# A competitive attention whose residual moves to ScalarE, whose counts are applied in the transposed copy, and whose steps stand in another order

## The reference, cut to what matters

```
x = x + tanh(g_xattn[1]) * L1_xattn(layernorm(x), ctx, alpha, beta)

def L1_xattn(X, C, alpha, beta):
    sim = sigmoid(beta + alpha * einsum('bkd,btd->bkt', C, X))
    mask = one_hot(argmax(sim, axis=1), K, axis=1)         # each token picks one context row
    agg = einsum('bkt,btd->bkd', sim * mask, X) + C         # what the tokens bring to their row
    out_k = agg / (sum(mask, axis=-1) + 1)                  # divided by one plus the count of tokens
    return X + einsum('bkt,bkd->btd', sim, out_k)
```

## Time and profile before

| what | value |
|---|---|
| time of 3 runs, median (lowest to highest) | 1693.77 us (1693.45 to 1694.56) |
| time of the profiled execution | 1691.46 us |
| span of its records | 1689.7 us |
| granted TensorE clock, mean of the span | 0.925 of full speed |
| busy share PE, VectorE, ScalarE, GpSimd | 83%, 64%, 40%, 46% |
| the phase | from about 453 to 557 us |

### The profile page before, as it was taken

One profiled execution on the slowest core, in us unless ns is written; L12 is line 12 of the kernel. 1 busy time (PEld: TensorE's weight loads), 2 busy tenths in 40 slices (PEclk: granted clock), 3 DMA queues, 4 the chain that ended last, 5 costly groups with the idle time before them and its releaser, 6 DMA issues. The chain is left out here.

```text
span 1689.7 us, 34140 instructions
## 1 busy us (share of the span) xinstructions
PE 1406.0 (83%) x10919; PEld 1116.2 (66%) x10919; DVE 1081.6 (64%) x2418; ACT 681.7 (40%) x1663; POOL 780.9 (46%) x1037
## 2 busy tenths in 40 slices
PE   4999765989656785999978886899999999687996
PEld 3777655989655564666634444777878778587884
DVE  4888752414399687999958884455555855364455
ACT  3676442323343333556633332344455454421121
POOL 2554581345384353555533331444444577307355
PEclk9999897999855897999979999899999999889899
DMA  6400015758110000000000000000000000186952
GB/s 183 179 2 2 11 34 158 220 170 265 54 33 10 1 1 1 0 0 0 0 1 0 0 0 1 1 0 0 0 1 1 6 20 15 54 235 188 275 163 83
DMA packets 96487, 100.03 MB, mean 59 GB/s; under 512 B 12150, under 2 KB 69678, under 8 KB 95727
## 3 DMA queue, kind: packets, MB, share of 16 engines
q1 hardware_dynamic: 62322, 69.60, 13.6%
q0 software_dynamic: 8192, 16.79, 3.4%
q10 hardware_dynamic: 25852, 12.09, 2.5%
HBM read 72.23 MB, written 26.21 MB: 58 GB/s over the span
## 5 line engine op out<-in xcount | busy, mean ns | idle before, releaser
L439 POOL TENSOR_TENSOR exp_scores<-exp_scores,softmax_recip 128x308 f32<-128x308 f32 x256 | 181.7, 742 | 179.8 <-DVE softmax_recip L611 179.6
L633 PE MATMUL psum<-identity,exp_scores 128*77 128x128 f32 x1024 | 164.7, 287 | 37.6 <-POOL exp_scores L439 25.4
L1942 POOL TENSOR_TENSOR exp_scores_xattn<-exp_scores_xattn,softmax_recip_xattn 128x1640 f32<-128x1640 f32 x32 | 93.5, 2921 | 162.6 <-DVE softmax_recip_xattn L2115 162.6
L1201 PE MATMUL psum<-sorted_transposed_ffn,tile_weights_up_ffn 128*128 128x128 f32 x1280 | 164.7, 283 | 4.3 <-DVE sorted_transposed_ffn L1089 4.1
L633 PEld LDWEIGHTS psum<-identity,exp_scores 128*77 128x77 f32 x1024 | 123.2, 153 | 60.5 <-issue 28.9
L1201 PEld LDWEIGHTS psum<-sorted_transposed_ffn,tile_weights_up_ffn 128*128 128x128 f32 x1280 | 154.1, 197 | 11.6 <-DVE sorted_transposed_ffn L1089 11.4
L975 POOL DMA_INDIRECT gathered_rows_ffn<-sorted_y,slot_ffn x96 | 90.7, 944 | 105.4 <-DMA sorted_y<-expert_rows_ffn 46.4
L454 ACT COPY probs_transposed<-psum 77x512 f32<-77x512 f32 x192 | 111.2, 581 | 57.3 <-PE psum L633 55.4
L1211 PE MATMUL psum<-expert_weights_down_ffn,hidden_ffn 128*128 x960 | 123.7, 280 | 3.3 <-issue 2.9
L964 POOL DMA_INDIRECT sorted_x<-xn_ffn,slot_ffn x64 | 61.3, 957 | 139.3 <-DVE slot_ffn L851 120.4
L1211 PEld LDWEIGHTS psum<-expert_weights_down_ffn,hidden_ffn 128*128 128x128 f32 x960 | 115.8, 195 | 5.2 <-issue 5.2
(11 more groups left out here) (367 smaller groups left out, 3388.7 us busy)
## 6 DMA issues: line engine op xcount, KB each, us to landing
tile_weights_up_ffn<-in_L_ffn_packed_dram SPq DMA_DIRECT2D x160, 256.0 KB, 3.3
sorted_rows_ffn<-sorted_x SPq DMA_DIRECT2D x80, 128.0 KB, 3.7
sorted_y<-expert_rows_ffn ACTq DMA_DIRECT2D x80, 128.0 KB
sorted_x<-zeros SPq DMA_DIRECT2D x4, 1280.0 KB, 13.0
x_residual<-in_x_dram SPq DMA_DIRECT2D x4, 512.0 KB, 11.3
expert_weights_down_ffn<-in_L_ffn_packed_dram SPq DMA_DIRECT2D x8, 256.0 KB, 15.2
sorted_x<-xn_ffn,slot_ffn POOLq DMA_INDIRECT x128, 2.2
gathered_rows_ffn<-sorted_y,slot_ffn POOLq DMA_INDIRECT x128, 2.9
```

The costliest lines, as they stand in the source:

```text
L439: nc.gpsimd.tensor_tensor(e[:, par, heads, :], e[:, par, heads, :], rec.to_broadcast([S, HG, KC]), ALU.mult).then_inc(s["probs_ready"], 1)
L633: last = nc.tensor.transpose(m.psum[0:KC, 4 + g % 2, h * S:(h + 1) * S], e[:, nxt, g * HG + h, :], m.ident[:, :])
L1201: mm = nc.tensor.matmul(m.psum[:, 2 * (n % 2) + half, to:to + SUB], w[:, n % DEPTH, u, at:at + 128], xst[:, n % 2, u * SUB:(u + 1) * SUB], ...
L1942: nc.gpsimd.tensor_tensor(ev, ev, recip[:, par, :].unsqueeze(2).to_broadcast([S, H3, KV]), ALU.mult).then_inc(s["probs_ready"], 1)
```

## The change

Four things are changed. (1) GpSimd no longer forms gate x xn and adds it. Since xn is rstd x x + shift, x + gate x xn is (1 + gate x rstd) x x + gate x shift; VectorE makes the two columns from rstd and shift (`moves`), and ScalarE applies them to x in place, right behind xn and for the group that it just normalised. (2) VectorE no longer multiplies `rows` by the reciprocal counts. ScalarE applies these as a scale while it copies the transposed sim out of PSUM: the counts belong to the partitions there, but differ by batch, so the one copy becomes four ACTIVATEs; it also moves behind the copy of the transposed xn. (3) On VectorE the small steps on the counts stand between the steps of the picks, and `combine` stands ahead of adding y to x. (4) On PE the transposes of sim stand ahead of the aggregation.

```diff
-                        wait(pool, s["x_moved"], g)
-                        nc.gpsimd.tensor_tensor(gated[:, :], xn[:, par, :, :].rearrange("p b d -> p (b d)"), m.gate[:, 1:2].to_broadcast([S, GB * D]),
-                                                ALU.mult).then_inc(s["xn_used"], 1)
-                        wait(pool, s["xn_used"], g + 1)
-                        xg = m.x[:, bass.ds(g * GB, GB), :].rearrange("p b d -> p (b d)")
-                        nc.gpsimd.tensor_tensor(xg, xg, gated[:, :], ALU.add).then_inc(s["x_moved"], 1)
...
                     if front:
                         wait(act, s["xt_in_psum"], g)
-                        wait(act, s["xn_used"], g)
+                        wait(act, s["weighted_ready"], g)
...
-                    if back:
-                        wait(act, s["simt_in_psum"], g)
-                        wait(act, s["y_done"], g - 1)
-                        nc.scalar.copy(simt[:, :], m.psum[0:KC, 2, :]).then_inc(s["simt_ready"], 1)
+                        wait(act, s["xn_ready"], g + 2)
+                        for t in range(GB):
+                            at = (g + 1) * GB + t
+                            ins = nc.scalar.activation(m.x[:, at, :], m.x[:, at, :], ACT.Identity, scale=move_scale[:, bass.ds(at, 1)],
+                                                       bias=move_shift[:, bass.ds(at, 1)])
+                        ins.then_inc(s["x_moved"], 1)
                     if front:
                         wait(act, s["xt_in_psum"], g + 2)
                         wait(act, s["z_in_psum"], g)
                         nc.scalar.copy(xt[:, nxt, :], m.psum[:, 0, :]).then_inc(s["xt_ready"], 1)
+                    if back:
+                        wait(act, s["simt_in_psum"], g)
+                        wait(act, s["y_done"], g - 1)
+                        wait(act, s["back_link"], (g - 1) * BACK + 2)
+                        for t in range(GB):
+                            ins = nc.scalar.activation(simt[:, t * S:(t + 1) * S], m.psum[0:KC, 2, t * S:(t + 1) * S], ACT.Identity,
+                                                       scale=tally[:, t // 2, t % 2:t % 2 + 1])
+                        ins.then_inc(s["simt_ready"], 1)
...
+                def moves(lo, hi):
+                    nc.vector.tensor_scalar(move_scale[:, lo:hi], m.rstd[:, lo:hi], gate, 1.0, ALU.mult, ALU.add).then_inc(s["moves_ready"], 1)
+                    nc.vector.tensor_scalar(move_shift[:, lo:hi], m.shift[:, lo:hi], gate, None, ALU.mult).then_inc(s["moves_ready"], 1)
...
-                        nc.vector.tensor_tensor(rows[:, :, :], rows[:, :, :], tl.unsqueeze(2).to_broadcast([KC, GB, D]), ALU.mult)\
-                            .then_inc(s["back_link"], 1)
...
+                    if g >= 0:
+                        combine(g)
                     if back:
                         wait(dve, s["y_done"], g)
                         wait(dve, s["x_moved"], g)
...
                         for t in range(GB):
                             nc.vector.bn_stats(m.moments[:, (g - 1) * GB + t, :], m.x[:, (g - 1) * GB + t, :])
-                    if g >= 0:
-                        combine(g)
...
                     if back:
+                        wait(pe, s["sim_ready"], g)
+                        wait(pe, s["simt_ready"], g - 1)
+                        for t in range(GB):
+                            mm = nc.tensor.transpose(m.psum[0:KC, 2, t * S:(t + 1) * S], sim[:, nxt, t, :], m.ident[:, :])
+                        mm.then_inc(s["simt_in_psum"], 1)
                         wait(pe, s["pick_ready"], g)
                         wait(pe, s["weighted_ready"], g)
...
                         mm.then_inc(s["agg_in_psum"], 1)
-                        wait(pe, s["simt_ready"], g - 1)
-                        for t in range(GB):
-                            mm = nc.tensor.transpose(m.psum[0:KC, 2, t * S:(t + 1) * S], sim[:, nxt, t, :], m.ident[:, :])
-                        mm.then_inc(s["simt_in_psum"], 1)
```

More of the change, by code:

```diff
@@ L1302, in competitive_attention @@
     names = ("parts_ready var_ready sd_ready rstd_ready shift_ready neg_ready ones_ready xn_ready xt_in_psum xt_ready "
-             "z_in_psum exp_ready one_added xn_used x_moved best_ready weighted_ready sim_ready pick_ready simt_in_psum simt_ready agg_in_psum y_done x_done mid_link back_link late_first late_combined late_moments")
+             "z_in_psum exp_ready one_added moves_ready x_moved best_ready weighted_ready sim_ready pick_ready simt_in_psum simt_ready agg_in_psum y_done x_done mid_link back_link late_first late_combined late_moments")
     s = {n: sem(f"{n}_1") for n in names.split()}
     gate = m.gate[:, 1:2]
-    MID, BACK = 3, 4
+    MID, BACK = 3, 3
     FIRST = 4
@@ L1328, in competitive_attention @@
         code = sb("pick_code", [S, GB])
-        gated = sb("gated_xn", [S, GB * D])
+        move_scale, move_shift = sb("one_plus_gated_rstd", [S, B]), sb("gated_shift", [S, B])
         weighted = sb("weighted_tokens", [S, 2, GB, D + 1])
@@ L1376, in _ @@
                 act.wait_ge(s["neg_ready"], 1)
-                act.wait_ge(s["shift_ready"], 1)
+                act.wait_ge(s["moves_ready"], 2)
                 def step(g, par, front, middle, back):
@@ L1385, in step @@
                         preload(nc, m, ACT.Exp)
-                        act.wait_ge(s["shift_ready"], before + 1)
+                        act.wait_ge(s["moves_ready"], 2 * before + 2)
                     if front:
                         wait(act, s["xt_in_psum"], g)
-                        wait(act, s["xn_used"], g)
+                        wait(act, s["weighted_ready"], g)
                         for t in range(GB):
@@ L1446, in step @@
                         rstd_of_x(nc, m, dve, s["sd_ready"], s["rstd_ready"], s["shift_ready"], lo, hi, before)
+                        moves(lo, hi)
                     link_m = chain(dve, s["mid_link"], g, MID)
@@ L1452, in step @@
                         nc.vector.reciprocal(sv, sv).then_inc(s["sim_ready"], 1)
+                    agg = m.psum[0:KC, 3:5, 0:2 * (D + 1)].rearrange("p j (u c) -> p j u c", u=2)
                     if back:
                         wait(dve, s["agg_in_psum"], g)
-                        wait(dve, s["y_done"], g - 1)
-                        agg = m.psum[0:KC, 3:5, 0:2 * (D + 1)].rearrange("p j (u c) -> p j u c", u=2)
+                        wait(dve, s["simt_ready"], g - 1)
                         nc.vector.tensor_scalar(tally[:, :, :].unsqueeze(3), agg[:, :, :, D:D + 1], 1.0, None, ALU.add).then_inc(s["back_link"], 1)
-                        nc.vector.tensor_tensor(rows[:, :, :].rearrange("p (j u) d -> p j u d", u=2), agg[:, :, :, 0:D],
-                                                m.ctx[:, bass.ds((g - 1) * GB, GB), :].rearrange("p (j u) d -> p j u d", u=2), ALU.add)\
-                            .then_inc(s["back_link"], 1)
-                        wait(dve, s["back_link"], (g - 1) * BACK + 2)
-                        nc.vector.reciprocal(tl, tl).then_inc(s["back_link"], 1)
-                        wait(dve, s["back_link"], (g - 1) * BACK + 3)
-                        nc.vector.tensor_tensor(rows[:, :, :], rows[:, :, :], tl.unsqueeze(2).to_broadcast([KC, GB, D]), ALU.mult)\
-                            .then_inc(s["back_link"], 1)
                     if middle:
@@ L1470, in step @@
                         nc.vector.tensor_reduce(best[:, par, :], sv, AX.X, ALU.max).then_inc(s["best_ready"], 1)
+                    if back:
+                        wait(dve, s["back_link"], (g - 1) * BACK + 1)
+                        nc.vector.reciprocal(tl, tl).then_inc(s["back_link"], 1)
+                    if middle:
                         wait(dve, s["best_ready"], g + 1)
@@ L1474, in step @@
                         link_m(nc.vector.tensor_tensor(pv, sv, best[:, par, :].unsqueeze(2).to_broadcast(wide), ALU.is_ge))
+                    if back:
+                        wait(dve, s["y_done"], g - 1)
+                        nc.vector.tensor_tensor(rows[:, :, :].rearrange("p (j u) d -> p j u d", u=2), agg[:, :, :, 0:D],
+                                                m.ctx[:, bass.ds((g - 1) * GB, GB), :].rearrange("p (j u) d -> p j u d", u=2), ALU.add)\
+                            .then_inc(s["back_link"], 1)
+                    if middle:
                         link_m(nc.vector.tensor_tensor(pv, pv, m.down[:, 0:KC].unsqueeze(1).to_broadcast(wide), ALU.mult))
```

1 line of the change is left out of this document (added).

## The result

The changed kernel took 1684.53 us (median of 5, 1681.15 to 1686.09) against 1693.45 (5, 1691.23 to 1694.56): ratio 0.9947, 95% interval 0.9931 to 0.9962. It is 8.9 us faster, where 10.3 (1683.5 us) had been worked out.

What follows compares the result with a forecast made beforehand. The phase was read as VectorE's time line, with 12.3 us standing still for GpSimd. Terms 7.45 + 2.1 - 0.1 + 0.8 + 0.45 - 0.24 - 0.2 gave 10.3 us less: 1683.5 us at the median, range 1679.5 to 1690.

Steps and rivals of the forecast that it cites:

- Rival 3: In rounds 1, 2, 4 any GpSimd work, gathers too, holds VectorE; 4.65 us would come back: 1688.2 us; 9%.
- rival 5: In rounds 1 to 4 combine operations are held beside their round's gathers, up to 22.8 us: 1706 us, slower; 5%.
- Rounds 0, 1, 2, 4: 12.2 us of holds, combine and small steps go, 4.75 stay or come: 7.45 us saved.
- Round 4's race: Comparison against GpSimd's L1356: 0.15 us of hold stays if comparison starts first, 0.95 if not; middle 0.55 taken.
- The wait for gathers in round 1: With combine ahead of L1482, VectorE comes for the sixth gather at 8.6, it lands at 10.0: 1.4 us wait.
- Round 3: VectorE does its combine inside the wait for PE; round falls from 11.98 to 9.9 us: 2.1 saved.
- Round 5: Hangs on the same chain to y as round 3, but has no combine: 0.1 us lost.
- Round 7: Scaled copies take 1.2 us, y is late next; round takes 7.65 us: 0.8 saved.
- Round 6: PE has all its work at the low clock, 8.0 us: 0.45 saved from 8.45.
- Rival 2: PE goes to 2.4 GHz in late rounds as it becomes denser, some 4 us: 1679.5 us; 12%.
- Start and tail: First copy 0.24 us later; tail's aggregation behind four transposes and y, 0.2 us lost.
- the rule weighed in the prediction: VectorE instructions with two SBUF inputs and GpSimd instructions reading SBUF exclude one another; the first issued keeps the other out.

Runs made afterwards that it cites:

- Experiments 1: Kernel before with only the residual moved from GpSimd to ScalarE, old steps and order kept: 1689.74 us, ratio 0.9974.
- 3: Changed kernel with two GpSimd additions of zeros, which nothing waits for, behind each product of xn and the maximum: 1693.28 us, ratio 0.9999 to the kernel before.
- 4: Changed kernel with two GpSimd memsets, which only write, behind each product of xn and the maximum: 1688.4 us, measured once.
- experiment 7: Changed kernel measured and profiled a second time, nothing edited: 1681.94 us, ratio 0.9938 to the kernel before.
- experiment 11: Changed kernel with x moved last on ScalarE, and y and scaled copies ahead of z and the xt copy after the first STATS only: 1683.79 us.
- experiment 6: Changed kernel with one plain copy of the transposed sim for the four scaled ones, leaving out division by counts: 1681.15 us, measured once.

## Why the prediction was right, point by point

The mechanism held: VectorE stood still for GpSimd's reads of SBUF, and with two of three operations gone it doesn't. Experiments 1, 3 and 4 show it: fewer reads, more reads, and work without reads. Rival 3 (any work of GpSimd holds VectorE) and rival 5 (combine held beside gathers) fall: the combine took 343 ns an operation beside the gathers. That the total came as near as 11.2 against 10.3 is in part luck, since the terms below miss in both directions, and PE's level alone moves the phase by 2.0 (experiment 7).

- **Rounds 0, 1, 2, 4:** 8.27 us saved against 7.45. Round 0's hold stayed, at 0.80 instead of 1.2; round 2's was 0.21 instead of 1.2: the last pick arrived near the end of L1356's time there, and experiment 11 shows 0.73 at another alignment. Round 4's race was won, 0.11 instead of the middle of 0.55: the small reciprocal runs in the gap before the comparison, so the margin is 0.04 as it was. The wait for gathers in round 1 was mis-sized the other way, 2.14 instead of 1.4:

```profile
479.43 0.35 DVE L1438 SCALAR_TENSOR_TENSOR x_residual<-gathered_rows_ffn,expert_weight_ffn,x_residual 128x128 f32<-128x128 f32 x1 [2.14 <-DMA gathered_rows_ffn<-sorted_y,slot_ffn]
```
```profile
470.26 1.11 POOL L1346 DMA_INDIRECT gathered_rows_ffn<-sorted_y,slot_ffn  x1 [1.93 <-DVE x_residual L1443]
...
476.94 0.95 POOL L1346 DMA_INDIRECT gathered_rows_ffn<-sorted_y,slot_ffn  x1 [0.30 <-issue]
```

VectorE came at 477.29, 8.6 after the picks' end, as worked out; the first gather started 1.6 after it instead of 1.3, and the six followed each other at 1.34 us instead of 1.25.
- **Round 3:** 2.07 against 2.1. L1495 started 8.33 after the reciprocal, as forecast. **Round 5:** 0.08 lost against 0.1. **Round 7:** 0.79 against 0.8, with scaled copies of 1.13 (1.2 was taken) and y as late as worked out. That it hung on the copies alone was not so (experiment 6): the sum of rows ends with them, 0.09 earlier.
- **Round 6:** 0.84 against 0.45. The sum took this round to be bound by PE, with all its work at 1.2 GHz. That step failed: the transposes of xn and z ran at the higher level (0.60 and 1.12 us), PE was done early and waited 0.90 us for VectorE's sum of rows, and the round went as round 7 did: VectorE adds y 6.03 us after the reciprocal, 6.08 in round 7. Rival 2 has the higher level come with the change; but in round 6 of the kernel before, the same two took 0.77 and 1.12 already, and y 1.32. In the second execution more of y ran at it.
- **Start and tail:** 0.66 lost against 0.44.
- **From the phase to the time:** 11.2 us in the first profile, 13.3 in the second; 8.9 and 11.2 in the two medians (1693.45 to 1684.53, 1693.10 to 1681.94). The term that I did not have is this: the profiled execution of before had later phases of 1132.8 us, the lowest of all profiles, which hides some of the gain in the two spans. Of the kernel before there is one profile only, so how far its own phase varies is not shown. What sets the level of PE's clock in the later phases from one execution to the next stays open.

## What to carry to other kernels

An engine can cost its neighbour more by reading SBUF beside it than by anything that waits for it: look for operations of one shape with different durations, and for what ends shortly (here 0.34 us) before the long ones do. Two edits can be worth more together than apart when the first clears the place into which the second moves work. Before one of two inputs of a product is shortened, see when the other one arrives, and before a late step is pulled ahead, who stands behind the step that it passes. And before an edit of one or two microseconds is judged by a profile, compare the stretches that the edit does not touch.

## What the runs showed of the hardware that was not expected

- A held VectorE operation can stay out across several GpSimd operations: 3.71 us through three of them, where 0.48 is its own time (experiment 3). In other rounds of the same run it got in between.
- TensorE's level in the same stretch of the same kernel differs between two executions, 0.63 and 0.70 granted between 520 and 546 us, and moves the phase by 2.0 us: as much as several of the edits tried here.
- A hold can begin before the record of the GpSimd operation behind it: 0.31 us in the earlier trace rows, and 0.50 in experiment 4 (VectorE, GpSimd), where both follow a gather without a gap. There the operation recorded first is the one that waits, which the rule weighed in the prediction does not explain. Why is open; a lead and a gather alone don't decide it, for in round 2 of the changed kernel a pick that started 0.20 ahead of L1356, which also stood right behind a gather, was not held (the last two rows).

```profile
477.26 1.70 DVE L1442 SCALAR_TENSOR_TENSOR x_residual<-gathered_rows_ffn,expert_weight_ffn,x_residual 128x128 f32<-128x128 f32 x1 [0.62 <-DMA gathered_rows_ffn<-sorted_y,slot_ffn]
```
```profile
476.79 0.94 POOL L1347 DMA_INDIRECT gathered_rows_ffn<-sorted_y,slot_ffn  x1 [0.30 <-issue]
477.76 1.05 POOL L1357 TENSOR_TENSOR weighted_tokens_xattn<-xn_xattn,best_sim_xattn 128x512 f32<-128x512 f32 x1
```
```profile
486.35 0.46 DVE L1486 TENSOR_TENSOR pick_xattn<-pick_xattn,descending_count 128x308 f32<-128x308 f32 x1
```
```profile
486.55 1.17 POOL L1356 TENSOR_TENSOR weighted_tokens_xattn<-xn_xattn,best_sim_xattn 128x512 f32<-128x512 f32 x1
```
